# Attention with a deferred softmax normalisation and an earlier weight-quantisation schedule, one post-LN layer on 8 cores

## Chip, cores and metric

One Trainium2 chip, one program on all 8 NeuronCores. The time is device microseconds of the slowest core. The cores share no data while the kernel runs: cores 0 to 3 work on batch element 0, cores 4 to 7 on batch element 1, and each core owns 2048 of the 8192 tokens of its element.

## What is computed

One transformer layer with the layer norm behind each residual sum:

```python
qkv = x @ w_qkv + b_qkv                      # x: (2, 8192, 2048), 16 heads of 128
scores = einsum('bqhd,bkhd->bhqk', q * SCALE, k)
attn = softmax(scores, axis=-1)
out = einsum('bhqk,bkhd->bqhd', attn, v)
x = layernorm(x + out @ w_proj + b_proj)

def quantize(w):                              # ternary weights
    gamma = mean(abs(w))                      # one number for the whole matrix
    return clip(round(w / (gamma + 1e-8)), -1, 1)
hidden = sigmoid(x @ quantize(w1).T) * (x @ quantize(w2).T)
x = layernorm(x + hidden @ quantize(w3).T)
```

w1 and w2 are 5632x2048, w3 is 2048x5632. The quantised weights depend on nothing that attention computes, so the kernel prepares them beside attention.

## The kernel before

Everything is written in raw engine programs: each phase is a block with one instruction stream per engine (tensor, scalar, vector, gpsimd, sync), and the order within a stream is the order of the code. Engines meet only at semaphores (t_a, t_b, t_c, t_q raised by TensorE, s_a by ScalarE, v_a, v_b, v_q, v_q2 by VectorE, and one ring per stream of DMAs). A block starts with `barrier`, which makes an engine wait for every count of the earlier blocks, the rings of DMAs included.

Phases in order: K and V projections for all 8192 tokens (to HBM scratch kscr, vscr), Q projection of the core's 2048 tokens (into qtsb), attention, output projection with layer norm, then the feed-forward part in two halves of 1024 tokens.

Attention (lines 540 to 773) runs over 16 heads h and, in each, two query halves qp of 1024 queries: 32 groups, g = 2h + qp. A group goes through 64 key chunks kc of 128 keys. TensorE makes the scores of a chunk (line 638, two matmuls of 512 columns into one of two tiles ps_s), ScalarE takes the exponential (line 696, ps_s to exs), and TensorE multiplies it with V (line 649, into po) and sums it with a column of ones (line 653, into row 0 of pl), always one chunk behind the scores. The last chunk's four matmuls are lines 660 and 663.

At the end of a group the sums are inverted and spread over the partitions. VectorE takes two reciprocals (lines 707, 708: pl to rlsb). TensorE spreads them with a one-row matmul (line 669) into ps_s[0]. VectorE copies that to rbsb (line 711) and multiplies both halves of po with it (line 714, into qtsb), raising v_b. Only then may TensorE start the next group, whose kc = 0 waits for v_b (line 634). ps_s, po and pl together fill PSUM, and the tiles pl have one partition each.

The weights are quantised on VectorE between groups, in 136 chunks of 128 rows by 2048 (or 1536) columns, in two passes. Pass 1 sums absolute values (line 724, L724 in the profile, wbuf2 to racc) of 17 chunks behind the second group of each of the heads 0 to 7. At the end of head 7 the totals give the three factors gi3, through two tiny matmuls (lines 677, 681), and TensorE may start head 8 only when they are there (line 626, v_q at NQ + 3). Pass 2 quantises (lines 754, 758, 762) 17 chunks behind the second group of each of the heads 8 to 15, and GpSimd stores them. GpSimd issues the loads of both passes three ahead of VectorE. SyncE loads K and V of a head two heads ahead.

The change touches the PSUM tiles pl, the lists q1_of_h and q2_of_h, and the attention streams of TensorE and VectorE. GpSimd's, ScalarE's and SyncE's streams stay as they are.

## Time and profile before

| | us |
|---|---|
| runs, median of 2 | 10211.64 (9977.26 to 10446.01) |
| the profiled execution's own time | 9977.26 |
| its span on the slowest core (core 0) | 9975.7 |
| spans of the eight cores | 9926.5 to 9975.7 |
| TensorE busy, core 0 | 8313.6 (83% of the span) |
| ScalarE busy | 2833.3 (28%) |
| VectorE busy | 2009.4 (20%) |

The page counts a matmul as busy from its start to its modelled end. The engines work side by side, so the shares don't add up to 100%. What stands in the row of a stage says more than the mean over the whole span, since the stages have different limits. Times within the text are microseconds from the start of the span of core 0.

### The profile page before, as it was taken

The page shows a single profiled execution, that of the slowest core. Times are in us where ns is not written, and L with a number is a line of the kernel's source. Part 1 is how long each engine was busy: PE and PEld are TensorE (multiplying, and loading weights), DVE is VectorE, ACT ScalarE, POOL GpSimd, SP SyncE. Part 2 cuts the span into 40 slices and gives each one's busy share as a digit, 9 for nine tenths or more (in the row PEclk, how much of TensorE's full clock was granted, in tenths as well). Part 3 has the DMA queues.
Part 4 walks back from the last instruction along what each step waited for, and adds up shares of the span by engine and source line. Part 5 has one row for each costly group of instructions (what it writes and reads, how often), then busy time and mean ns, then how long its engine had stood idle before and what let it go on. Part 6 is the DMA issues. An engine that isn't in the chain of part 4 may idle for free. (4 is left out here: it accounts for less than half of the span.)

```text
span 9975.7 us, 92282 instructions; the slowest of 8 cores (9926.5 to 9975.7 us)
## 1 busy us (share of the span) xinstructions
PE 8313.6 (83%) x31982; PEld 2850.2 (29%) x31982; DVE 2009.4 (20%) x1975; ACT 2833.3 (28%) x2856; POOL 730.0 (7%) x1119
## 2 busy tenths in 40 slices
PE   6999699988999999979999999956499876399773
PEld 2444244432222222222222222212144322144221
DVE  1111111111222222220333333343300001100002
ACT  1111111123555555545555555510000000000000
POOL 2111111100000000000111111111100000000000
PEclk9999899999999999989999999978799999699997
DMA  5333433443222222220333333279733222533223
GB/s 88 69 69 70 83 70 72 75 67 64 89 89 87 85 83 83 75 82 21 125 125 125 125 125 117 98 145 123 114 78 79 49 71 65 124 77 68 56 70 103
DMA packets 1174111, 868.24 MB, mean 87 GB/s; under 512 B 925857, under 2 KB 1056929, under 8 KB 1140897
## 3 DMA queue, kind: packets, MB, share of 16 engines
q0 software_dynamic: 312704, 488.71, 21.6%
q1 hardware_dynamic: 860962, 373.62, 15.2%
q8 instruction: 276, 4.52, 0.2%
q14 instruction: 169, 1.38, 0.1%
HBM read 679.52 MB, written 186.65 MB: 87 GB/s over the span
## 5 line engine op out<-in xcount | busy, mean ns | idle before, releaser
L696 ACT ACTIVATE exs<-ps_s,negc 128x1024 bf16<-128x1024 f32 x2048 | 2278.6, 1114 | 1800.5 <-PE ps_s L638 1800.4
L649 PE MATMUL po<-exs,vh 128*128 128x512 bf16 x4032 | 1583.0, 393 | 17.4 <-ACT exs L696 17.4
L653 PE MATMUL pl<-exs,ones_bf 128*1 128x512 bf16 x4032 | 1546.3, 384 | 0.0
L638 PE MATMUL ps_s<-qtsb,kh 128*128 128x512 bf16 x4096 | 1287.1, 399 | 116.4 <-DVE qtsb L714 86.1
L270 PE MATMUL pk<-xg,wkv 128*128 128x512 bf16 x4096 | 928.9, 381 | 153.2 <-DMA xg<-xb 153.2
L1183 PE MATMUL px<-hidden,w3t 128*128 128x512 bf16 x2816 | 708.7, 386 | 242.8 <-DMA w3t<-w3qs 240.2
L298 PE MATMUL pv<-wkv,xg 128*128 128x512 bf16 x4096 | 894.6, 380 | 10.4 <-DVE vsb L346 10.4
L1060 PE MATMUL px<-ysbh,w1t 128*128 128x512 bf16 x2816 | 626.1, 381 | 215.7 <-DMA w2t<-w2qs 215.7
L653 PEld LDWEIGHTS pl<-exs,ones_bf 128*1 128x1 bf16 x4032 | 318.6, 79 | 1220.7 <-issue 1220.7
L316 ACT ACTIVATE ksb<-pk,bkrs 128x512 bf16<-128x512 f32 x256 | 176.0, 687 | 1666.2 <-PE pk L270 1485.2
L649 PEld LDWEIGHTS po<-exs,vh 128*128 128x128 bf16 x4032 | 391.1, 97 | 896.8 <-issue 889.3
L707 DVE RECIPROCAL rlsb<-pl 1x512 f32<-1x512 f32 x32 | 107.1, 3346 | 2652.6 <-PE pl L663 2652.6
L1069 PE MATMUL px<-ysbh,w2t 128*128 128x512 bf16 x2816 | 622.1, 379 | 0.0
L270 PEld LDWEIGHTS pk<-xg,wkv 128*128 128x128 bf16 x4096 | 386.5, 98 | 641.5 <-issue 207.4
L298 PEld LDWEIGHTS pv<-wkv,xg 128*128 128x128 bf16 x4096 | 399.0, 98 | 498.4 <-issue 25.6
L1183 PEld LDWEIGHTS px<-hidden,w3t 128*128 128x128 bf16 x2816 | 242.2, 98 | 716.0 <-issue 524.3
L1060 PEld LDWEIGHTS px<-ysbh,w1t 128*128 128x128 bf16 x2816 | 276.3, 98 | 553.6 <-issue 224.2
L638 PEld LDWEIGHTS ps_s<-qtsb,kh 128*128 128x128 bf16 x4096 | 241.0, 99 | 645.2 <-issue 645.2
L1085 ACT ACTIVATE s1s<-px 128x1024 bf16<-128x1024 f32 x88 | 90.1, 1024 | 1097.5 <-PE px L1069 1097.4
L61 POOL DMA_DIRECT2D xg<-xb x512 | 272.0, 634 | 1551.1 <-PE pv L298 1538.5
L335 DVE TENSOR_REDUCE knmax<-pn 1x1 f32<-1x512 f32 x256 | 173.8, 679 | 1025.0 <-PE pn L281 988.2
L1069 PEld LDWEIGHTS px<-ysbh,w2t 128*128 128x128 bf16 x2816 | 275.5, 98 | 332.2
(118 smaller groups left out, 3943.4 us busy)
## 6 DMA issues: line engine op xcount, KB each, us to landing
wbuf<-w POOLq DMA_DIRECT2D x240, 1024.0 KB, 7.6
xg<-xb POOLq DMA_DIRECT2D x512, 128.0 KB, 7.3
kscr<-ksb SPq DMA_DIRECT2D x256, 128.0 KB, 1.8
vscr<-vsb SPq DMA_DIRECT2D x1024, 32.0 KB, 1.6
kh<-kscr SPq DMA_DIRECT2D x16, 2048.0 KB, 8.0
wp<-wproj POOLq DMA_DIRECT2D x64, 512.0 KB, 9.8
wbuf<-w POOLq DMA_DIRECT2D x32, 768.0 KB, 7.7
w1qs<-wqb POOLq DMA_DIRECT2D x44, 512.0 KB, 5.5
```

The source lines that it names most:

```text
L61: e.dma_start(out=out, in_=in_, **kw).then_inc(cc.h, 16)
L270: mm = e.matmul(pk[idx % 2][:], wkv[:, dc * 2048 + h_l * 128:dc * 2048 + (h_l + 1) * 128], xg[s % 2][:, dc * 512:(dc + 1) * 512], start=(d ...
L298: mm = e.matmul(pv[jdx % 2][:], xg[s % 2][:, dc * 512 + kc * 128:dc * 512 + (kc + 1) * 128], wkv[:, dc * 2048 + 1024 + g4l * 512:dc * 2048 ...
L316: e.activation(ksb[idx % 2][:], pk[idx % 2][:], AF.Identity, bias=bkrs[:, h:h + 1], scale=RS)
L335: rm = e.reduce_max(knmax[0:1, col:col + 1], pn[idx % 2][0:1, :], axis=AX)
L638: mm = e.matmul(ps_s[kc % 2][:, q2 * 512:(q2 + 1) * 512], kh[h % 2][:, kc * 128:(kc + 1) * 128], qtsb[:, h * TOK + qp * 1024 + q2 * 512: h ...
L649: e.matmul(po[q2][:], vh[h % 2][:, p * 128:(p + 1) * 128], exs[p % 4][:, q2 * 512:(q2 + 1) * 512], start=(p == 0), stop=False)
L653: mm = e.matmul(pl[q2][0:1, :], ones_bf[:, 0:1], exs[p % 4][:, q2 * 512:(q2 + 1) * 512], start=(p == 0), stop=False)
L696: s_a.inc(e.activation(exs[kc % 4][:], ps_s[kc % 2][:], AF.Exp, bias=negc[:, h:h + 1]))
L1060: e.matmul(px1[jc % 2][:, q2 * 512:(q2 + 1) * 512], w1t[jg % 2][:, dc * 512 + jc2 * 128: dc * 512 + jc2 * 128 + 128], ysbh[:, dc * 1024 + ...
L1069: mm = e.matmul(px2[jc % 2][:, q2 * 512:(q2 + 1) * 512], w2t[jg % 2][:, dc * 512 + jc2 * 128: dc * 512 + jc2 * 128 + 128], ysbh[:, dc * 10 ...
L1183: mm = e.matmul(px3[dcw][:, q2 * 512:(q2 + 1) * 512], w3t[n % 4][:, dcw * 128:(dcw + 1) * 128], hidden[:, hc * 1024 + q2 * 512: hc * 1024 ...
```

## The change

Four edits, all within attention:

1. The tiles pl get 128 partitions instead of one. They keep their two PSUM banks.
2. The matmuls that spread the reciprocals of group g write into pl and no longer into ps_s[0], and they stand in the next group: behind its scores of kc = 0 and kc = 1. The wait for v_b moves there too, ahead of the first product with V. Groups 13 and 31 are exceptions. Group 13's spread stands at the end of head 6 (there line 682), group 31's behind the last head.
3. VectorE copies pl to rbsb in two pieces of 512 columns instead of one of 1024.
4. Pass 1 takes 23, 23, 23, 23, 22 and 22 chunks behind heads 0 to 5, the factors are made at the end of head 6, and pass 2 takes 17 chunks behind each of the heads 7 to 14.

```diff
-                pl = [... psum_tensor(f"pl{i}", [1, 512], F32))
+                pl = [... psum_tensor(f"pl{i}", [128, 512], F32))
...
-                q1_of_h = [list(range(h_ * 17, (h_ + 1) * 17)) if h_ < 8 else []
-                           for h_ in range(H)]
-                q2_of_h = [list(range((h_ - 8) * 17, (h_ - 7) * 17)) if h_ >= 8
-                           else [] for h_ in range(H)]
+                _q1c = [23, 23, 23, 23, 22, 22] + [0] * 10
...
+                q2_of_h = [list(range((h_ - 7) * 17, (h_ - 6) * 17))
+                           if 7 <= h_ <= 14 else [] for h_ in range(H)]
...
-                            if h == 8:
+                            if h == 7:
                                 e.wait_ge(v_q.h, b[v_q] + NQ + 3)
...
-                                    if kc == 0 and g >= 1:
-                                        e.wait_ge(v_b.h, b[v_b] + g)
...
+                                    if kc == 1 and g >= 1:
+                                        if g != 14:
+                                            e.wait_ge(v_a.h, b[v_a] + g)
+                                            for q2 in range(2):
+                                                mm = e.matmul(
+                                                    pl[q2][:], ones_fr[0:1, :],
+                                                    rlsb[0:1, q2 * 512:(q2 + 1) * 512],
+                                                    start=True, stop=True)
+                                            t_c.inc(mm)
+                                        e.wait_ge(v_b.h, b[v_b] + g)
...
-                                e.wait_ge(v_a.h, b[v_a] + g + 1)
-                                for q2 in range(2):
-                                    mm = e.matmul(ps_s[0][:, q2 * 512:(q2 + 1) * 512],
...
-                            if h == 7:
+                            if h == 6:
+                                e.wait_ge(v_a.h, b[v_a] + 14)
...
                                 e.wait_ge(v_q.h, b[v_q] + NQ + 1)
-                                e.wait_ge(v_b.h, b[v_b] + 16)
...
-                                vsync(e, e.tensor_copy(rbsb[:], ps_s[0][:]))
+                                e.tensor_copy(rbsb[:, 0:512], pl[0][:])
+                                vsync(e, e.tensor_copy(rbsb[:, 512:1024],
+                                                       pl[1][:]))
...
-                                if h == 7:
+                                if h == 6:
```

TensorE between groups 0 and 1, before: the last four products of group 0, the spread of the reciprocals (from rlsb), the scores of the next group (ps_s, from kh0), and its first product.

```order
L660 MATMUL po1<-exs3,vh0 128x512
L663 MATMUL pl1<-exs3,ones_bf 1x512
L669 MATMUL ps_s0<-rlsb,ones_fr 128x512 [waits v_a]
L669 MATMUL ps_s0<-rlsb,ones_fr 128x512
L638 MATMUL ps_s0<-qtsb,kh0 128x512 [waits v_b]
L638 MATMUL ps_s0<-qtsb,kh0 128x512
L638 MATMUL ps_s1<-qtsb,kh0 128x512 x2
L649 MATMUL po0<-exs0,vh0 128x512 [waits s_a]
```

The same place after the change.

```order
L672 MATMUL po1<-exs3,vh0 128x512
L675 MATMUL pl1<-exs3,ones_bf 1x512
L640 MATMUL ps_s0<-qtsb,kh0 128x512 x2
L640 MATMUL ps_s1<-qtsb,kh0 128x512 x2
L651 MATMUL pl0<-rlsb,ones_fr 128x512 [waits v_a]
L651 MATMUL pl1<-rlsb,ones_fr 128x512
L661 MATMUL po0<-exs0,vh0 128x512 [waits v_b,s_a]
```

The four matmuls of the scores have moved ahead of the spread and wait for nothing, and the wait for v_b now stands on the first product with V.

VectorE at the end of attention, before: the last group's copy and products (rbsb, qtsb), then the first of 17 chunks of pass 2 (gi: the factors, tq and wqb: the quantised chunk).

```order
L711 COPY rbsb<-ps_s 128x1024 [waits t_c]
L714 TENSOR_TENSOR qtsb<-po,rbsb 128x512 [waits v_s]
L714 TENSOR_TENSOR qtsb<-po,rbsb 128x512
L754 TENSOR_SCALAR tq<-wbuf_2,gi 128x2048 [waits v_b,r_q22,r_q2s1]
L758 TENSOR_SCALAR tq<-wbuf_2,gi 128x2048 [waits v_s]
L762 TENSOR_TENSOR wqb_1<-tq 128x2048 [waits v_s]
```

The same place after the change.

```order
L727 COPY rbsb<-pl 128x512 [waits t_c]
L728 COPY rbsb<-pl 128x512
L732 TENSOR_TENSOR qtsb<-po,rbsb 128x512 [waits v_s]
L732 TENSOR_TENSOR qtsb<-po,rbsb 128x512
L577 UNCONDITIONAL_BRANCH [waits v_b]
```

No chunk of pass 2 is left behind the last group, and the block ends there.

## Rows read from the trace of the kernel before

**Rows 1.** Stages, core 0: us; PE, PEld, DVE, ACT, POOL busy; clock, DMA share, GB/s.

```profile
2385.00:4525.00 2140.00, 1875.36 (x6281) 506.10 (x6281) 453.90 (x257) 1153.16 (x1037) 73.83 (x139) 0.90 0.27 86
...
6520.00:6640.00 120.00, 15.32 (x58) 5.93 (x59) 65.30 (x59) 3.35 (x4) 33.18 (x37) 0.56 0.76 208
```

**Rows 2.** Timeline of core 0 around the end of group 6.

```profile
3296.39 3.35 DVE L707 RECIPROCAL rlsb<-pl 1x512 f32<-1x512 f32 x1 [58.32 <-PE pl L663]
...
3303.09 3.75 PE L669 MATMUL ps_s<-rlsb,ones_fr 1*128 1x512 f32 x4 [6.81 <-DVE rlsb L708]
...
3306.95 1.22 DVE L711 COPY rbsb<-ps_s 128x1024 f32<-128x1024 f32 x1 [4.00 <-PE ps_s L669]
...
3309.71 1.86 PE L638 MATMUL ps_s<-qtsb,kh 128*128 128x512 bf16 x4 [2.87 <-DVE qtsb L714]
...
3312.08 0.58 PE L649 MATMUL po<-exs,vh 128*128 128x512 bf16 x1 [0.50 <-ACT exs L696]
```

**Rows 3.** The reciprocal that opens each group's end: groups 7, 15 and 16.

```profile
3422.61 3.35 DVE L707 RECIPROCAL rlsb<-pl 1x512 f32<-1x512 f32 x1 [113.05 <-PE pl L663]
4432.73 3.35 DVE L707 RECIPROCAL rlsb<-pl 1x512 f32<-1x512 f32 x1 [112.96 <-PE pl L663]
4614.95 3.35 DVE L707 RECIPROCAL rlsb<-pl 1x512 f32<-1x512 f32 x1 [112.29 <-PE pl L663]
```

**Rows 4.** Stretch of core 0, TensorE alone: busy, granted clock, DMA share, GB/s.

```profile
3318.00:3320.00 2.00, 2.00 (x8) 0.96 0.00 0
```

**Rows 5.** Scores of four chunks of group 7, two at each clock level.

```profile
3314.16 1.03 PE L638 MATMUL ps_s<-qtsb,kh 128*128 128x512 bf16 x2
...
3317.12 1.03 PE L638 MATMUL ps_s<-qtsb,kh 128*128 128x512 bf16 x2
...
3319.31 0.60 PE L638 MATMUL ps_s<-qtsb,kh 128*128 128x512 bf16 x2
...
3321.00 0.60 PE L638 MATMUL ps_s<-qtsb,kh 128*128 128x512 bf16 x2
```

**Rows 6.** The stall at the end of head 7: VectorE, then TensorE.

```profile
4497.74 1.75 DVE L724 TENSOR_REDUCE racc<-wbuf 128x1 f32<-128x1536 f32 x1 [0.31 <-DMA wbuf<-w]
...
4503.13 1.87 PE L638 MATMUL ps_s<-qtsb,kh 128*128 128x512 bf16 x4 [0.73 <-DVEq L748]
```

**Rows 7.** The end of attention and the start of the output projection, core 0.

```profile
6508.20 3.35 DVE L707 RECIPROCAL rlsb<-pl 1x512 f32<-1x512 f32 x1 [113.10 <-PE pl L663]
...
6520.09 1.29 DVE L714 TENSOR_TENSOR qtsb<-po,rbsb 128x512 bf16<-128x512 f32 x2
...
6602.44 0.96 DVE L762 TENSOR_TENSOR wqb<-tq 128x1536 bf16<-128x1536 bf16 x1
...
6612.44 45.42 SPq L61 DMA_DIRECT2D xm<-xm  x9
6622.67 11.99 PE L877 MATMUL pp<-qtsb,wp 128*128 128x512 bf16 x48 [104.02 <-DMA wp<-wproj]
```

**Rows 8.** The start of attention, core 0: last copy before it, first load, first product.

```profile
2395.73 0.17 DVE L499 COPY negc<-pnc 128x16 f32<-128x16 f32 x1 [0.82 <-PE pnc L504]
2397.09 0.32 SPq L61 DMA_DIRECT2D kh<-kscr  x1
...
2428.81 0.59 PE L649 MATMUL po<-exs,vh 128*128 128x512 bf16 x1 [1.78 <-ACT exs L696]
```

**Rows 9.** The end of group 0.

```profile
2539.06 3.35 DVE L707 RECIPROCAL rlsb<-pl 1x512 f32<-1x512 f32 x1 [143.16 <-PE pl L663]
```

**Rows 10.** Stretches as in the fourth group, at the starts of attention and of the projection.

```profile
2434.00:2436.00 2.00, 2.00 (x8) 0.97 1.14 217
6624.00:6626.00 2.00, 2.00 (x7) 0.58 1.72 161
```

**Rows 11.** Pass 1 behind head 0: first and last chunk.

```profile
2678.43 2.29 DVE L724 TENSOR_REDUCE racc<-wbuf 128x1 f32<-128x2048 f32 x1 [0.18 <-DVE qtsb L714]
...
2730.61 2.29 DVE L724 TENSOR_REDUCE racc<-wbuf 128x1 f32<-128x2048 f32 x1 [0.27 <-DMA wbuf<-w]
```

**Rows 12.** Groups by form: a VectorE copy of 512 columns out of PSUM.

```profile
L189 DVE COPY bvb<-pstp 128x512 f32<-128x512 f32 x4 | 2.8, 692 | 9.6 <-PE pstp L181 9.6
```

More of the change, by code:

```diff
@@ L566, in build @@
                 NW = 44 * 128 * 2048
-                q1_of_h = [list(range(h_ * 17, (h_ + 1) * 17)) if h_ < 8 else []
-                           for h_ in range(H)]
-                q2_of_h = [list(range((h_ - 8) * 17, (h_ - 7) * 17)) if h_ >= 8
-                           else [] for h_ in range(H)]
+                _q1c = [23, 23, 23, 23, 22, 22] + [0] * 10
+                q1_of_h = []
+                _qa = 0
+                for h_ in range(H):
+                    q1_of_h.append(list(range(_qa, _qa + _q1c[h_])))
+                    _qa += _q1c[h_]
+                q2_of_h = [list(range((h_ - 7) * 17, (h_ - 6) * 17))
+                           if 7 <= h_ <= 14 else [] for h_ in range(H)]
                 b = snap()
@@ L683, in _ @@
                                                  start=True, stop=True))
+                        e.wait_ge(v_a.h, b[v_a] + 32)
+                        for q2 in range(2):
+                            mm = e.matmul(pl[q2][:], ones_fr[0:1, :],
+                                          rlsb[0:1, q2 * 512:(q2 + 1) * 512],
+                                          start=True, stop=True)
+                        t_c.inc(mm)
                     @blk.scalar
```

9 lines of the change are left out of this document (5 added, 4 removed).

## The prediction

> **What bounds the kernel now.** I read the spans of the cores first: all eight lie within 50 us of each other, so core 0 stands for the chip. Then I read the stages. In the first half of attention TensorE is busy for 1875 of 2140 us, ScalarE for 1153 and VectorE for 454 [rows 1], and the second half looks alike, so TensorE's order of work sets the time there, and only what lets TensorE start sooner, or run at the higher of its two clock levels for longer, can pay. Behind attention comes a stretch of 120 us in which TensorE has 15 us of work and its granted clock is 0.56 of full speed [rows 1].
>
> The timeline gives three kinds of gap within attention. The first stands at the end of every group [rows 2]. Behind the last matmul of group 6 TensorE idles 6.81 us for the two reciprocals, spreads them for 3.75 us, idles 2.87 us for copy and products, makes four scores matmuls (1.86 us), and waits 0.50 us for the exponential. The first product with V starts at 3312.08, which is 15.69 us after the reciprocal's start at 3296.39. The second gap is at the end of head 7: from one reciprocal to the next it takes 182.22 us [rows 3] instead of the usual 126.22 (3296.39 to 3422.61) [rows 2, 3]. TensorE can't begin head 8 before 4503.13, because 17 chunks of pass 1 and the factors stand ahead of it on VectorE [rows 6]. The third is the tail: the last group's products end at 6521.38, then come 17 chunks of pass 2 to 6603.40, then the stores must land, and the next phase's first load is issued at 6612.44 [rows 7].
>
> The 32 reciprocals lie between 2539.06 and 6508.20 [rows 7, 9]. That is 3969.14 us in 31 intervals. Without the long one there remain 3786.92 us in 30 intervals, or 126.23 us each.
>
> **The group boundary.** Edit 2 leaves the chain of reciprocals, spread, copy and products as it is, and takes the four scores matmuls and the wait for the first exponential from behind it. They now run while the reciprocals are taken. The first product with V can start where the scores start now, 13.32 us after the reciprocal's start (3309.71 less 3296.39) [rows 2]. Queued behind the new wait for the reciprocals is only work that needs po or pl, both of which VectorE still reads; ScalarE has both exponentials done within the 6.81 us. Nothing is delayed by the move.
>
> Edit 3 turns a copy of 1.22 us [rows 2] into two of 512 columns. One such copy alone takes 0.69 us [rows 12], so two take 1.38 at most. The pair of products of the same width takes 1.29 [rows 7]. I take 0.1 us more. The bounds are 0.07 and 0.16, under 3 us of difference over all groups. By the Trainium skill (VectorE: DVE Perf Modes, "The TRN2 errata"), each instruction out of PSUM pays a fixed 120 cycles, an estimate of 0.13 us for the second copy. The rows' bounds, 0.07 and 0.16, lie around that; the sum would be 1 us less of a gain by it. With my 0.1 the first product starts 13.4 us after the reciprocal.
>
> How long is it from the first product to the next reciprocal? The trace has one group that starts just as all will after the change, with both exponentials ready: group 0. Its first product starts at 2428.81 [rows 8] and its reciprocal at 2539.06 [rows 9]: 110.25 us. So an interval would be 13.4 + 110.25 = 123.65 us.
>
> A part of this is the clock. After each gap TensorE runs at 1.2 GHz for a while. At group 6's end the clock comes back just after 3318 (0.96 over 3318 to 3320) [rows 4], 8.4 us after the restart at 3309.71 and 6 us after the first product. In group 0 it came back just after 2434 [rows 10], 5.3 us after the first product. At the projection's start, with matmuls in one unbroken row from 6622.67 [rows 7], it came back within 3.3 us (0.58 over 6624 to 6626) [rows 10]. The low clock costs 0.43 of its time here: a chunk takes 2.96 us (3314.16 to 3317.12) instead of 1.69 (3319.31 to 3321.00) [rows 5]. I expect 3.5 to 5.5 us of it after a restart without the half-microsecond pause, towards the short end, which makes 109.5 to 110.3 us, and take 109.6. The interval is then 13.4 + 109.6 = **123.0 us**. The bounds are 122.7 and 124.2 (a return 6.8 us after the product).
>
> The rule of the Trainium skill (TensorE: Matmul & The Clock Gate, "What's actually happening") is that the slow state is the default and recent activity releases it. By that rule it is the unbroken row of matmuls that counts, and the trace agrees: 3 to 5 us in the unbroken row and 8.4 us with the pause of 0.50 us in it.
>
> By the moved work alone, 15.69 less 13.4, the gain would be 2.3 us an interval; the rest of my 3.2 is the shorter low clock, as group 0 and the projection's start show it.
>
> The gain is 126.23 − 123.0 = 3.2 us in 30 intervals, **97 us** (61 to 106 by the bounds).
>
> **The end of head 6.** The stall moves to group 13, with no chunk ahead of it. There VectorE ends its products 13.3 us after the reciprocal. The three totals, two tiny matmuls and factors take what they take now, from 4499.49 (4497.74 + 1.75) to 4503.13, 3.64 us [rows 6]. Since TensorE waits for them before head 7, its scores stay behind the chain here: 1.87 + 0.50 us more until the first product. 13.3 + 3.6 + 2.4 + 110 makes 129.3 us. Against 182.2 this gains **53 us** (51 to 54).
>
> What must hide the 17 chunks that stood there is the 113 us that VectorE is idle in a group [rows 3]. Pass 1 takes 54.5 us for 17 chunks (2678.43 to 2732.90) [rows 11], 3.2 us each, so 23 take 74 us. Even without the three that are loaded ahead it is 77. Some 39 us are left before the next reciprocal. The loads share the DMA queues with K and V of a later head in the kernel before too, so their pace already has that in it. If that cover were gone, each us over it would stall TensorE six times.
>
> **The tail.** Pass 2 ends behind head 14, where the 82 us of its 17 chunks (6521.38 to 6603.40 in the tail now) [rows 7] fit into the same 113 us. The last group's products are then the last work of the block. From there to the first load of the next block it is now 91.06 us (6521.38 to 6612.44) [rows 7]. The start of attention shows what such a change of blocks takes with nothing outstanding: 1.2 us from the end of the copy (2395.90) to the first load (2397.09) [rows 8]. Gain: **90 us** (85 to 91). What is late next is the load of w_proj, 10.2 us from the first issue to the first matmul (6612.44 to 6622.67) [rows 7], as before. Nothing in the later phases changes.
>
> **Sum.** 97 + 53 + 90 = 240 us. The profiled execution took 9977.26 us, its span being 9975.7, so the forecast is **9738 us**. The median of the two runs shown, 10211.64, lies 234 us above that execution, half-way to a run of 10446. I predict against the profiled one.
>
> **Rivals.**
>
> 1. The low clock stays as long after a restart as it does now, 8.4 us from the first matmul. Then an interval is 13.4 + 108.0 + 0.43 x 8.4 = 125.0 us, where 108.0 is 110.25 less 0.43 x 5.3. Only 37 us come from the boundaries, 180 in all: 9797 us. For it speaks that the four matmuls ahead of the chain and the spread still leave pauses of some 6 and 3 us; against it, group 0 [rows 8 to 10].
> 2. A part of the 90 us comes back. If the eight cores reach the projection closer together and its weight loads slow each other, or the cores that now finish early wait, half of the gain could go: 9783 us. Against it: all cores show the same stages now, and DMA was already at 0.76 in the tail [rows 1].
> 3. Slower: the 23 chunks don't fit. VectorE takes the next reciprocal late, and TensorE, which in a group's end waits for nothing else, stalls in six groups. To eat the other gains, each of the six stalls must be 40 us, so that 23 chunks take 153 us, 6.6 us a chunk. The measured pace is 3.2 [rows 11], and it starts to matter at 4.9 us. At 7 us a chunk the time would be 9738 + 6 x (161 − 113), or 10026 us.
>
> **How the numbers follow.** The forecast gets 0.72, rival 1 0.14, rival 2 0.11, and rival 3 0.03. The forecast's bounds reach from about 9724 (all gains at their upper end) to 9781, and executions differ by some 0.3%, 30 us. With rivals 1 and 2 the range is 9700 to 9800. A change of 2% is about what a measurement of this kernel can tell from none; here it is 200 us, so faster means under 9778 us. The forecast lies 40 us on that side, rival 1 on the other, and rival 2 on the edge. That gives 0.82 for faster, 0.15 for within 2%, and 0.03 for slower.
>
> **What would show it.** In the profile after: about 123 us between reciprocals; TensorE's four scores matmuls directly behind a group's last product; the first product with V about 13.4 us behind the reciprocal's start, and the clock back within 5.5 us of it; one interval of about 129 us between groups 13 and 14 and none of 182; the first load of the projection 1 to 2 us behind VectorE's last product; pass 1 done some 75 us behind each of six heads. The prediction is wrong if the intervals stay above 124.5 us, if a reciprocal waits for a chunk of pass 1, or if TensorE's idle time before the projection is above 30 us.

## The result, and the profile after

| | before | after |
|---|---|---|
| median of all runs, us | 10426.7 (13 runs) | 10214.23 (14 runs) |
| lowest, us | 9977.26 | 9734.5 |
| ratio after / before | | 0.9746, 95% interval 0.9726 to 0.9766 |
| span of core 0 in the profiled execution, us | 9975.7 | 9733.8 |

The changed kernel is faster by 2.5%. The forecast was 9738. The comparison rests on five executions of after, from 9734.5 to 9750.51 us, and three of before, from 9977.26 to 10012.81, since in all the others, which set both medians, the cores of one die or both ran at a lower granted clock, as they did in many executions of the experiments too (the two longest, the first of one_ahead and the first of ones128, took 16385 and 23688 us). The profile of after comes from an execution of 10238.4 us, whose late cores are 4 to 7. All rows of after below are from core 0, whose span was 9733.8 us and whose mean granted clock was 0.932.

On core 0 the gain is 9975.7 − 9733.8 = 241.9 us; I had summed 240. It is divided as follows.

The end of a group comes first. This is the timeline of core 0 of after around the end of group 2; the rows are those of [rows 2] in their new order, and the last is the next group's reciprocal.

```profile
2776.77 1.04 PE L640 MATMUL ps_s<-qtsb,kh 128*128 128x512 bf16 x4
2776.94 3.35 DVE L723 RECIPROCAL rlsb<-pl 1x512 f32<-1x512 f32 x1 [35.49 <-PE pl L675]
...
2783.64 3.75 PE L651 MATMUL pl<-rlsb,ones_fr 1*128 1x512 f32 x4 [5.84 <-DVE rlsb L724]
...
2787.50 0.69 DVE L727 COPY rbsb<-pl 128x512 f32<-128x512 f32 x1 [4.00 <-PE pl L651]
2788.11 0.68 DVE L728 COPY rbsb<-pl 128x512 f32<-128x512 f32 x1
2788.89 1.29 DVE L732 TENSOR_TENSOR qtsb<-po,rbsb 128x512 bf16<-128x512 f32 x2
...
2790.43 0.58 PE L661 MATMUL po<-exs,vh 128*128 128x512 bf16 x1 [3.04 <-DVE qtsb L732]
...
2899.68 3.35 DVE L723 RECIPROCAL rlsb<-pl 1x512 f32<-1x512 f32 x1 [109.51 <-PE pl L675]
```

The four scores matmuls start directly behind the group's last product, at the high clock (1.04 us for four, where they took 1.86 behind the chain). The chain of reciprocals, spread, copies and products is as long as it was. The first product with V no longer waits for an exponential: it is released by VectorE's products. It starts 2790.43 − 2776.94 = 13.49 us after the reciprocal, where it was 15.69. From it to the next reciprocal, at 2899.68, it takes 109.25 us. The interval is 122.74 us. Its mean over all boundaries but one is 122.9, where it was 126.23. Of these 3.3 us 2.2 come from the work that was moved (15.69 less 13.49) and 1.1 from the time between the first product and the next reciprocal (110.54 us before, 109.42 after, in the mean).

TensorE alone in short stretches of core 0 of after, as in [rows 4] (busy, granted clock, DMA share, GB/s).

```profile
2792.00:2794.00 2.00, 2.00 (x6) 0.52 0.00 0
```

The higher of the two clock levels, 2.4 GHz, is back at about 2793.9, which is 3.5 us after the first product (3.3 to 4.2 over the 30 boundaries of this kind). Before the change it was 6 us (5.1 to 6.4).

The whole of attention stands in one row of the view of one line, the first reciprocal of each group (duration in ns; first and last start).

```profile
L723 DVE RECIPROCAL rlsb<-pl x32: 3345/3346/3346, 2531.1 to 6347.4; 1x512 f32<-1x512 f32 x32
```

6347.4 − 2531.1 = 3816.3 us, against 3969.14 before [rows 7, 9]. One of the 31 intervals is the one behind head 6. Its ends, and what happens between, on core 0 of after:

```profile
4128.70 3.35 DVE L723 RECIPROCAL rlsb<-pl 1x512 f32<-1x512 f32 x1 [109.68 <-PE pl L675]
...
4145.28 1.86 PE L640 MATMUL ps_s<-qtsb,kh 128*128 128x512 bf16 x4 [0.63 <-DVEq L766]
...
4257.59 3.35 DVE L723 RECIPROCAL rlsb<-pl 1x512 f32<-1x512 f32 x1 [112.68 <-PE pl L675]
```

Here the totals follow VectorE's products at once, TensorE's scores wait for the factors as at the end of head 7 before [rows 6], and the interval is 128.89 us instead of 182.22. The other 30 share 3687.4 us, 122.9 each.

What had to hide the longer pieces of pass 1 still hides them: behind head 0 the first and the last of 23 chunks lie 74.0 us apart, from the first start to the last end, and the next reciprocal comes 35.5 us later (2741.45 to 2776.94), released by TensorE. The rows answer to [rows 11].

```profile
2667.45 2.29 DVE L742 TENSOR_REDUCE racc<-wbuf 128x1 f32<-128x2048 f32 x1 [0.18 <-DVE qtsb L732]
...
2739.16 2.29 DVE L742 TENSOR_REDUCE racc<-wbuf 128x1 f32<-128x2048 f32 x1 [0.63 <-DMA wbuf<-w]
```

The tail on core 0 of after, as in [rows 7].

```profile
6359.36 1.29 DVE L732 TENSOR_TENSOR qtsb<-po,rbsb 128x512 bf16<-128x512 f32 x2
6362.55 1.30 SPq L61 DMA_DIRECT2D xm<-xm  x3
...
6371.91 4.42 PE L895 MATMUL pp<-qtsb,wp 128*128 128x512 bf16 x10 [14.06 <-DMA wp<-wproj]
```

From the end of the last products, 6360.65, to the first load of the projection it is 1.9 us, where it was 91.06. TensorE's idle time before the projection fell from 104.02 to 14.06 us, and what ends it is still the load of w_proj. The stage of attention says the same, in the columns of [rows 1]: TensorE is busy for 1939 of 2140 us instead of 1875, at a mean clock of 0.93 instead of 0.90.

```profile
2377.00:4517.00 2140.00, 1939.44 (x6607) 529.19 (x6607) 529.61 (x332) 1213.16 (x1092) 101.58 (x173) 0.93 0.31 99
```

So 152.8 us come from between the first and the last reciprocal and 90.0 us from TensorE's idle time ahead of the projection, 243 together. The phases ahead of the first reciprocal were 8 us shorter, and those from the projection's first matmul to the end took 3361.9 us, 9 more than before. Both are within what the same code shows from one execution to the next, below.

### The profile page after: what moved, and what is told of

Read it like the earlier page. It is cut to its first block and busy times, and to the rows that moved or that the text cites. A ratio compares the mean times of both kernels' runs of the same rounds, so it can differ in the third digit from the quotient of the medians.

```text
span 10236.9 us, 92313 instructions; the slowest of 8 cores (9712.5 to 10236.9 us)
## 1 busy us (share of the span) xinstructions
PE 8770.1 (86%) x31982; PEld 2916.2 (28%) x31982; DVE 2010.8 (20%) x2007; ACT 2833.2 (28%) x2856; POOL 740.0 (7%) x1119
## 5 line engine op out<-in xcount | busy, mean ns | idle before, releaser
L661 PE MATMUL po<-exs,vh 128*128 128x512 bf16 x4032 | 1630.6, 404 | 93.5 <-DVE qtsb L732 91.2
L665 PE MATMUL pl<-exs,ones_bf 128*1 128x512 bf16 x4032 | 1589.0, 394 | 0.0
L270 PE MATMUL pk<-xg,wkv 128*128 128x512 bf16 x4096 | 1089.1, 429 | 148.8 <-DMA xg<-xb 148.8
L298 PE MATMUL pv<-wkv,xg 128*128 128x512 bf16 x4096 | 1051.5, 428 | 7.6 <-DVE vsb L346 7.6
L270 PEld LDWEIGHTS pk<-xg,wkv 128*128 128x128 bf16 x4096 | 420.4, 106 | 755.1 <-issue 689.2
L298 PEld LDWEIGHTS pv<-wkv,xg 128*128 128x128 bf16 x4096 | 435.5, 107 | 614.9 <-issue 530.9
L1103 ACT ACTIVATE s1s<-px 128x1024 bf16<-128x1024 f32 x88 | 90.2, 1024 | 1097.4 <-PE px L1087 1097.4
```

Of the source, the lines that this page charges most:

```text
L270: mm = e.matmul(pk[idx % 2][:], wkv[:, dc * 2048 + h_l * 128:dc * 2048 + (h_l + 1) * 128], xg[s % 2][:, dc * 512:(dc + 1) * 512], start=(d ...
L298: mm = e.matmul(pv[jdx % 2][:], xg[s % 2][:, dc * 512 + kc * 128:dc * 512 + (kc + 1) * 128], wkv[:, dc * 2048 + 1024 + g4l * 512:dc * 2048 ...
L661: e.matmul(po[q2][:], vh[h % 2][:, p * 128:(p + 1) * 128], exs[p % 4][:, q2 * 512:(q2 + 1) * 512], start=(p == 0), stop=False)
L665: mm = e.matmul(pl[q2][0:1, :], ones_bf[:, 0:1], exs[p % 4][:, q2 * 512:(q2 + 1) * 512], start=(p == 0), stop=False)
```

## The experiments

Times are of the profiled execution, and rows of core 0, where nothing else is said. "The reciprocals" are the first of each group, and their interval is the length of a group with its end. In the experiments from the pause on the lowest times of the unchanged kernel before, taken beside them on the same chips, were 9980 to 10006 us. Beside the first three its lowest was 10409.39 us, so their times aren't set against it, only their rows against those of the profile before.

### Each half of the change alone

**The schedule alone** (edit 4 in the kernel before; the chain stays as it was):

```diff
-                q1_of_h = [list(range(h_ * 17, (h_ + 1) * 17)) if h_ < 8 else []
+                _q1c = [23, 23, 23, 23, 22, 22] + [0] * 10
...
-                            if h == 8:
+                            if h == 7:
                                 e.wait_ge(v_q.h, b[v_q] + NQ + 3)
```

> The kernel before with the new schedule of the quantisation alone (edit 4). My theory, that the terms add and are independent: the intervals between reciprocals stay at 126.2 us, the one of 182.2 us becomes about 129.9 us (126.2 plus 3.6 for the factors), and the tail of 91 us becomes 2 us. That is 52 + 89 = 141 us less, some 1.4%. The rival theory, that the earlier passes of quantisation give something back (chunks that make a reciprocal late, or weight loads of the projection that collide), expects intervals behind heads 0 to 5 above 126.5 us or a projection that starts later, and less than 100 us in all.

**The deferred spread alone** (edits 1 to 3, the old lists):

```diff
-                                    if kc == 0 and g >= 1:
-                                        e.wait_ge(v_b.h, b[v_b] + g)
...
+                                    if kc == 1 and g >= 1:
+                                        if g != 16:
+                                            e.wait_ge(v_a.h, b[v_a] + g)
...
                             if h == 7:
+                                e.wait_ge(v_a.h, b[v_a] + 16)
```

> The kernel after with the old schedule of the quantisation (edits 1 to 3 alone). My theory: intervals of 122.9 us instead of 126.2 at 30 boundaries, 99 us less in all (1.0%), with the stall at the end of head 7 (182 us) and the tail (91 us) as before. If the clock came back no sooner after a restart than in the kernel before, and only the four scores matmuls and the wait for the exponential were saved, the intervals would be 123.9 to 125.0 us and the gain 37 to 70 us.

They took 9845.22 and 9883.4 us. The reciprocals of the two kernels, the schedule alone first.

```profile
L711 DVE RECIPROCAL rlsb<-pl x32: 3345/3346/3346, 2521.3 to 6432.1; 1x512 f32<-1x512 f32 x32
```

```profile
L719 DVE RECIPROCAL rlsb<-pl x32: 3344/3346/3346, 2540.1 to 6408.5; 1x512 f32<-1x512 f32 x32
```

With the schedule alone the intervals stay at 126.2 us, but for some of 124.0 to 125.9 behind groups 16 to 21, the one behind head 6 is 129.87, and TensorE's idle time ahead of the projection is 14.5 us instead of 104.0. Attention gains 58.3 us (3969.1 less 3910.8) and the tail 90. With the deferred spread alone all intervals but one are 122.9 us, and the stall behind head 7 stays, with an interval of 180.7. It gains 100.7 us in attention (3969.1 less 3868.4), where I had summed 97. The tail stays: TensorE is idle for 110.3 us ahead of the projection, 6 more than before.

The two gains in attention add up to 159 us; the whole change has 152.8. The 6 us that are left are the shorter intervals behind groups 16 to 21, which the whole change doesn't have. There the clock comes back sooner. This is the first product behind the end of group 17, and the clock around it.

```profile
4684.91 0.58 PE L653 MATMUL po<-exs,vh 128*128 128x512 bf16 x1 [0.50 <-ACT exs L700]
```

```profile
4684.00:4686.00 2.00, 1.50 (x4) 0.52 0.77 146
```

It is back 1.0 us after the first product here (0.52 over 4684 to 4686, and 1.00 from then on), and 3.0 to 5.7 us after it at the five other places, where most boundaries of this kernel have 5.8 to 6.4, all with the same matmuls and the same pause of 0.50 us. What brings it back sooner there is open. Otherwise the terms are independent, and each is where I had put it.

**Only the tail undone** (the change, with pass 2 behind heads 8 to 15 again):

```diff
-                q2_of_h = [list(range((h_ - 7) * 17, (h_ - 6) * 17))
-                           if 7 <= h_ <= 14 else [] for h_ in range(H)]
+                q2_of_h = [list(range((h_ - 8) * 17, (h_ - 7) * 17))
+                           if 8 <= h_ <= 15 else [] for h_ in range(H)]
```

> The kernel after with pass 2 behind heads 8 to 15 as before, pass 1 and the factors early. Theory: only the tail comes back, 89 us (stores of the last chunks included), and the intervals in attention stay at 122.9 and 128.9 us. The rival, that the early pass 2 costs something within attention (its loads and stores beside K and V), expects less than 89 us between the two kernels, by what the early pass had cost.

It took 9841.88 us. The projection's first matmuls:

```profile
6464.51 10.84 PE L895 MATMUL pp<-qtsb,wp 128*128 128x512 bf16 x39 [104.21 <-DMA wp<-wproj]
```

Attention is as long as with the whole change (3816.3 us). TensorE's idle time ahead of the projection is 104.21 again, 90.15 more than the 14.06 with the whole change. Core 0's span is 106.5 us longer, though, 14 of it in the phases behind, where the two kernels have the same code: 3375.8 us against 3361.9. Over all kernels of this part the same phases took 3351.8 to 3375.8 us. A difference of spans is thus uncertain by some 20 us, and that is why the terms are read from the places where they arise. Rival 2, by which a part of the 90 us comes back, has nothing for it but the 9 us by which these phases were longer in after than in before, and this kernel, with the old tail, has the longest of all.

### What brings the clock back

The forecast took 0.9 of the 3.2 us that it gave each boundary from a sooner return of the clock, and gave the matmuls' unbroken row behind the restart as the reason. Two kernels break the row or change its place.

**A pause put in** (the products of the second chunk wait for the third exponential):

```diff
-                                        e.wait_ge(s_a.h, eb + p + 1)
+                                        e.wait_ge(s_a.h,
+                                                  eb + (3 if p == 1 and kc == 2 else p + 1))
```

> The kernel after with a pause put back behind the restart: the second chunk's products with V wait for the third exponential, not only the second, so TensorE stops for about 1.5 us some 3 us after each group's first product. Theory, that only an unbroken row of matmuls brings the clock back: it comes back 6.5 to 8.5 us after the first product instead of 3.5, and the interval is 13.4 + 108 + 1.5 + 0.43 x (5.3 to 6.8) = 125.2 to 125.8 us. Rival, that the time after the restart alone decides: the clock is back 3.5 us after the first product in spite of the pause, and the interval is 124.1 us.

It took 9866.59 us. The end of group 2 on its core 0, then stretches of TensorE as above.

```profile
2784.11 3.35 DVE L723 RECIPROCAL rlsb<-pl 1x512 f32<-1x512 f32 x1 [37.05 <-PE pl L675]
...
2797.61 0.58 PE L661 MATMUL po<-exs,vh 128*128 128x512 bf16 x1 [3.04 <-DVE qtsb L732]
...
2802.08 0.58 PE L661 MATMUL po<-exs,vh 128*128 128x512 bf16 x1 [1.36 <-ACT exs L712]
...
2910.19 3.35 DVE L723 RECIPROCAL rlsb<-pl 1x512 f32<-1x512 f32 x1 [112.83 <-PE pl L675]
```

```profile
2806.00:2808.00 2.00, 2.00 (x7) 0.78 0.00 0
```

The chain is as in the change (13.50 us to the first product), the pause is 1.36 us long, and the interval is 126.08 us (126.2 in the mean). The clock is back at about 2806.9, 9.3 us after the first product and 4.8 us after the pause. At 29 of the 30 boundaries of this kind it is 9.0 to 9.6 us. So the rival, by which the return comes 3.5 us after the product whatever stands behind it, is refuted there. At the one behind group 14 the return is at 3.4 us and the interval 124.0 us, the rival's own numbers, with the same pause. The theory's direction is right for nearly all, and its size too small: it costs 3.3 us an interval, more than I expected. With 5.8 us more at the low clock, at 0.43 of the time, 2.5 us of it are the clock and some 0.8 the pause itself. Why the return takes 9.3 us and not the 6.5 to 8.5 of the expectation isn't settled.

**Less work ahead of the chain** (only the first chunk's scores are ahead; the second's follow the wait for v_b):

```diff
-                                    for q2 in range(2):
-                                        mm = e.matmul(
-                                            ps_s[kc % 2][:, q2 * 512:(q2 + 1) * 512],
...
-                                    t_a.inc(mm)
                                     if kc == 1 and g >= 1:
...
                                         e.wait_ge(v_b.h, b[v_b] + g)
+                                    for q2 in range(2):
+                                        mm = e.matmul(
+                                            ps_s[kc % 2][:, q2 * 512:(q2 + 1) * 512],
...
+                                    t_a.inc(mm)
```

> The kernel after, but only the scores of chunk 0 go ahead of the chain; those of chunk 1 stand behind the wait for v_b again, so that the restart is scores, then products, with no pause. Theory (unbroken row): the clock is back 3 to 6.8 us after the restart, the interval is 13.4 + 108.4 + 0.43 x (3.4 to 6.8) = 123.3 to 124.7 us. Rival, that what shortened the low clock was matmuls ahead of the chain, or that the restart must begin with products: the clock stays low for 8.4 us as in the kernel before, and the interval is 125.4 us.

It took 9772.9 us. The restart at the end of group 2 and the stretch in which the clock returns, then the same for group 5.

```profile
2784.03 1.01 PE L650 MATMUL ps_s<-qtsb,kh 128*128 128x512 bf16 x2 [2.94 <-DVE qtsb L732]
```

```profile
2786.00:2788.00 2.00, 2.00 (x6) 0.72 0.00 0
```

```profile
3152.98 1.01 PE L650 MATMUL ps_s<-qtsb,kh 128*128 128x512 bf16 x2 [2.94 <-DVE qtsb L732]
```

```profile
3157.00:3159.00 2.00, 2.00 (x5) 0.50 0.87 242
```

In the first the unbroken row begins with two scores matmuls at 2784.03, and the clock is back about 3.1 us later. At 25 boundaries it is back 2.9 to 4.7 us behind the restart, but at five, of which the second is one, 6.0 to 6.3 us, with an unbroken row there too; these five have the longest intervals, 124.3 to 124.6 us. The interval is 123.5 us in the mean, 0.6 above the change's, for 1 us more of work behind the restart. So most of the gain doesn't rest on how much stands ahead of the chain.

Counted from the restart alike, the return comes 3.3 to 4.2 us behind it in the change, 2.9 to 4.7 or 6.0 to 6.3 us here, and 3.0 us at the projection's start [rows 7, 10], all with nothing in between. Where a wait interrupts TensorE it is 8.4 us at the end of group 6 before (7.5 to 8.7 at the others) [rows 2, 4], 9.0 to 9.6 us with the longer pause, and 8.9 us in group 0, where four scores matmuls at 2425.16 and a wait of 1.78 us stand ahead of the first product [rows 8, 10]. Against this stand the one boundary of the pause kernel with 3.4 us and four of the schedule alone, with 3.4 to 6.7 us in spite of the wait. So an interruption mostly goes with a later return, but it isn't all that decides, and what else does wasn't tested. By the rule of the Trainium skill that the prediction weighed (TensorE: Matmul & The Clock Gate, "What's actually happening") recent activity releases the slow state; most of these boundaries agree, and the exceptions aren't explained by it as I used it.

### The cover of pass 1

**Pass 1 behind three heads** (45, 45 and 46 chunks), to test rival 3 where it must decide:

```diff
-                _q1c = [23, 23, 23, 23, 22, 22] + [0] * 10
+                _q1c = [45, 45, 46] + [0] * 13
```

> The kernel after with pass 1 in 45, 45 and 46 chunks behind heads 0 to 2. Theory: VectorE takes a chunk in 3.2 us as before, so 45 take 144 us where 109.6 us are idle; three intervals grow from 122.9 to about 158 us, 105 us more in all, all other intervals are unchanged. If the pace fell below that once the loads ran on without a break (the slower rival of the prediction), the three intervals would be above 170 us.

It took 10174.27 us. I read it on core 2, whose mean granted clock, 0.913, is the highest of the eight. There all intervals but three and the one behind head 6 are 122.7 to 123.8 us, close to the change's. Under the row stands what ends VectorE's wait before a reciprocal, and how often.

```profile
L723 DVE RECIPROCAL rlsb<-pl x32: 3345/3345/3346, 2675.7 to 6615.1; 1x512 f32<-1x512 f32 x32
its engine sat idle before it (us, times) until:
  PE pl L675: 2517.7, 29
  DVE racc L742: 0.8, 3
```

Three of 32 reciprocals are released by a chunk of pass 1, and not by TensorE: the stall that rival 3 described. Their intervals are about 163 us, 40 more (expected 158), and attention is 3939.4 − 3816.3 = 123 us longer. So the mechanism is real, at 45 chunks and 3.3 us a chunk. The change's 23 chunks take 74 of the 109.5 us that VectorE is idle in a group of the changed kernel (122.9 less 13.4), and they cost nothing.

### Past the change: the sums

What is left at a group's end is the chain itself. It exists because the sums stand in one partition: a matmul with a column of ones. With a 128 by 128 matrix of ones the sums stand in all partitions at once, and the spread and its copy aren't needed.

**Ones of 128 columns, the reciprocal straight from PSUM:**

```diff
-                                            mm = e.matmul(pl[q2][0:1, :],
-                                                          ones_bf[:, 0:1],
+                                            mm = e.matmul(pl[q2][:],
+                                                          ones_bb[:],
...
+                                e.reciprocal(rbsb[:, 0:512], pl[0][:])
+                                vsync(e, e.reciprocal(rbsb[:, 512:1024],
+                                                      pl[1][:]))
```

> The kernel after, with the sums taken by a 128x128 tile of ones instead of 128x1, so that they stand on all partitions and VectorE takes the reciprocals straight to rbsb: no spread, no copy. The chain to the first product falls from 13.4 to about 8.3 us. Theory (the chain is what bounds the boundary): intervals of 118 us if loading 128 columns of ones costs TensorE nothing more, 120.5 us if the 19 ns by which the two weight loads differ (98 and 79 ns) come on top in each of the 128 products of a group. Rival, that the bound is elsewhere: intervals stay near 122.9 us or rise.

It took 9084.55 us (another execution 9075.62), and attention 3164.1 from first to last reciprocal. The chain at one group's end:

```profile
2738.65 3.36 DVE L703 RECIPROCAL rbsb<-pl 128x512 f32<-128x512 f32 x1 [15.25 <-PE pl L668]
...
2745.32 1.29 DVE L708 TENSOR_TENSOR qtsb<-po,rbsb 128x512 bf16<-128x512 f32 x2
```

The chain is 8.0 us long instead of 13.4, as reckoned; the reciprocal of 512 columns takes 3.36 us whether in 1 or 128 partitions. But the intervals are 101 to 102.4 us, not 118 to 120.5. Some 16 us a group more went than the shorter chain accounts for. That asked for a kernel with the ones alone.

**Ones of 128 columns, and nothing else** (the chain, the spread and the copies stay as in the change):

```diff
-                                            mm = e.matmul(pl[q2][0:1, :],
-                                                          ones_bf[:, 0:1],
+                                            mm = e.matmul(pl[q2][:],
+                                                          ones_bb[:],
```

> The kernel after with the sums taken by the 128x128 tile of ones, and nothing else: reciprocals of row 0, spread and copies stay. The run with ones on 128 columns and a shorter chain had intervals of 102 us where 118 to 120.5 were expected. Theory: the rest came from the product's weights. With weights of one column a matmul starts 0.31 us after the one before it, with 128 columns throughout 0.22 us, so a chunk falls from 1.69 to about 1.43 us and the interval by 64 x 0.26 = 16.6 us, to 106.3 us. Rival, that the shorter chain alone did it (an idle time short enough for the clock to stay up for most of the boundary): the interval stays at 122 to 123 us.

It took 9238.45 us.

```profile
L725 DVE RECIPROCAL rlsb<-pl x32: 3344/3345/3347, 2513.4 to 5831.8; 1x512 f32<-1x512 f32 x32
```

3318.4 us, or 107 an interval; most of the saving is in the steady row of matmuls and has nothing to do with the boundary. The theory had 106.3, and the rival, the shorter chain alone, 122 to 123. The shorter chain is worth the other 5 us (107 here, 102 in the version before). A chunk within a group, in the timeline with the weight loads (PEld), first of the changed kernel and then of this one:

```profile
3001.07 0.38 PE L661 MATMUL po<-exs,vh 128*128 128x512 bf16 x1
...
3001.37 0.08 PEld L665 LDWEIGHTS pl<-exs,ones_bf 128*1 128x1 bf16 x1 [0.24 <-issue]
3001.38 0.38 PE L665 MATMUL pl<-exs,ones_bf 128*1 128x512 bf16 x1
3001.68 0.10 PEld L661 LDWEIGHTS po<-exs,vh 128*128 128x128 bf16 x1 [0.23 <-issue]
```

```profile
3001.25 0.38 PE L663 MATMUL po<-exs,vh 128*128 128x512 bf16 x1
3001.25 0.10 PEld L667 LDWEIGHTS pl<-exs,ones_bb 128*128 128x128 bf16 x1
3001.47 0.38 PE L667 MATMUL pl<-exs,ones_bb 128*128 128x512 bf16 x1
3001.47 0.10 PEld L663 LDWEIGHTS po<-exs,vh 128*128 128x128 bf16 x1
```

In the first, these loads stand at the start of their own matmuls, behind the matmul before, and a matmul and its neighbour start 0.31 us apart where one of the two has the single column. The two others of the six steps of a chunk, from scores to scores and from scores to the first product, are 0.22 us long in the steady row of this kernel too. In the second kernel a load stands one matmul ahead, under the one that is running, and all of them can start 0.215 us apart. A chunk takes 1.43 us in the mean instead of 1.69, and 64 chunks of 0.26 us less make the 16 us. The mean is over 6 x 0.215 = 1.29 us since TensorE now often waits for ScalarE ahead of the first product, which then starts 0.15 us behind the end of the exponential. That step is mostly 0.27 or 0.44 us long, and in the stretch shown chunks take 1.30 and 1.56 us in turn. "Busy" doesn't show it: the duration printed for one matmul is 0.38 to 0.39 us in both.

**The reciprocal off the path** (ones of 128 columns; VectorE copies pl and po out of PSUM, raises v_b, and inverts and multiplies in SBUF beside the next group):

```diff
+                                    e.tensor_copy(
+                                        rbsb[:, q2 * 512:(q2 + 1) * 512],
+                                        pl[q2][:])
...
+                                    mm = e.tensor_copy(
+                                        pob[:, q2 * 512:(q2 + 1) * 512],
+                                        po[q2][:])
+                                v_b.inc(mm)
+                                e.wait_ge(v_b.h, v_b.n)
+                                vsync(e, e.reciprocal(rbsb[:], rbsb[:]))
```

> The kernel after with the sums on all partitions (128x128 ones) and the normalisation off TensorE's path: VectorE copies pl and po out of PSUM (four copies of 512 columns, 2.6 us) and raises v_b; reciprocal and product follow in SBUF while the next group runs. The first product comes about 2.9 us behind the last one of the group before plus the scores, so TensorE idles 2 us instead of 5.8 + 3.0. If the clock then stays high, the intervals are 2.9 + 108 = 111 us, and 113.4 with a slower weight load; if it still falls, about 2 us more. That is 9.5 to 12 us less in 31 intervals than in the kernel after, about 9740 - 330 = 9410 us. Rival: the clock falls at each boundary and stays low as long as now, or the longer work of VectorE behind v_b (8 us) makes pass 1 or 2 late; then the intervals are 115 us or more and the time is above 9500 us.

Its two best executions took 8913.27 and 8924.95 us; the rows are of core 0 of another, with a span of 8897.7 us. A group's end, then TensorE in the stretch behind the end of the group before it and behind this one.

```profile
2988.82 1.29 DVE L705 COPY rbsb<-pl 128x512 f32<-128x512 f32 x2 [85.46 <-PE pl L669]
...
2991.41 6.55 DVE L714 RECIPROCAL rbsb<-rbsb 128x1024 f32<-128x1024 f32 x1
...
2991.56 0.38 PE L655 MATMUL po<-exs,vh 128*128 128x512 bf16 x1 [1.98 <-ACT exs L693]
```

```profile
2897.00:2899.00 2.00, 1.78 (x6) 0.50 0.00 0
...
2991.00:2993.00 2.00, 1.44 (x7) 1.00 0.92 377
```

The boundary costs TensorE 1.98 us of idle time. Behind this one the clock doesn't fall (1.00), but that is the exception: at 20 of the 24 boundaries with this idle time it falls behind the restart, as at the one before (0.50 over 2897 to 2899), and is back 3.5 to 4.7 us after the first product. Where it falls the interval is mostly 95.7 to 95.9 us, at the four where it doesn't 94.0 to 94.2. The expectation, 9410 us, was made before the effect of the ones was known. From the 107 us of ones_only the first product's earlier start takes 10.75 us (2.74 us behind the first copy instead of 13.49), and the shorter low clock some 0.4, which makes the measured 95.7. Behind the heads 7 to 11, though, the intervals are 101 to 102 us, and VectorE's timeline at one of these shows why:

```profile
4251.83 1.22 DVE L761 TENSOR_TENSOR wqb<-tq 128x2048 bf16<-128x2048 bf16 x1
4253.23 1.29 DVE L705 COPY rbsb<-pl 128x512 f32<-128x512 f32 x2 [0.17 <-DVE wqb L761]
```

The copy out of PSUM is released by a chunk of pass 2, and no longer by TensorE: rival 3's mechanism. 17 of the wide chunks take 89 to 91 us there, 65 of them work, and most of the rest waits for the stores; with VectorE's 11 us at the group's end that is more than 95.7. Behind heads 12 to 14, with narrower chunks in them, they take 83 to 85 us, and these intervals stay at 94.2 to 95.9 us.

**The chunks spread over all groups** (12 or 11 of pass 1 behind groups 0 to 11, 8 of pass 2 behind groups 14 to 30, the factors behind group 13):

```diff
-                _q1c = [23, 23, 23, 23, 22, 22] + [0] * 10
+                _q1c = [12] * 4 + [11] * 8 + [0] * 20
...
+                q2_of_g = [list(range((g_ - 14) * 8, (g_ - 13) * 8))
+                           if 14 <= g_ <= 30 else [] for g_ in range(2 * H)]
```

> The kernel with copies out of PSUM and the normalisation off the path, and the chunks of pass 1 and 2 spread over all groups (12 or 11 behind groups 0 to 11, 8 behind groups 14 to 30) instead of every other one. In the run before it the intervals were 95.7 us, but some 102 us in pass 2: there 17 chunks (82 us) and VectorE's own 11.5 us leave nothing of 95.7. Theory: all intervals but the one with the factors are 95.7 us and attention takes 30 to 40 us less than before, some 8870 us in all. Rival, that the loads and stores of pass 2 themselves slow the groups: intervals between 96 and 100 us in every group of pass 2, and no gain.

It took 8886.93 us, spans of 8836.4 to 8885.4. Attention from the first copy to the last, and what ends VectorE's wait before it.

```profile
L705 DVE COPY rbsb<-pl x64: 678/686/692, 2513.8 to 5482.6; 128x512 f32<-128x512 f32 x64
its engine sat idle before it (us, times) until:
  PE pl L669: 1662.2, 32
```

All 32 are released by TensorE, the intervals are 93.9 to 96.0 us (108.9 at the factors), and attention takes 39 us less than in the version before (3007.1 to 2968.2, from the first copy of the first group to that of the last). The rival, intervals of 96 to 100 us all through pass 2, is refuted. This version beats both kernels: its 8886.93 us is 1090 below the lowest time of before and 848 below the lowest of after. It is one execution, so no interval stands beside it.

## Why the prediction was right, and where it was not

**The group boundary: right.** "With my 0.1 the first product starts 13.4 us after the reciprocal": 13.49. "I expect 3.5 to 5.5 us of it after a restart, towards the short end": 3.5. "Which makes 109.5 to 110.3 us, and take 109.6": 109.25. The interval came out at 122.9 instead of 123.0, and 30 of them gained 100 us instead of 97. I had divided the 3.2 us of an interval into 2.3 for the moved work and 0.9 for the clock; they are 2.2 and 1.1 of 3.3. The price of the low clock, 0.43 of its time, is borne out by the schedule alone: at the boundary shown the clock is back 5.2 us sooner than at most, and the interval is 124.0 us, 2.2 less. Rival 1 (125.0 us) is refuted by the same rows. The reason that I gave for the sooner return, the unbroken row, holds at most boundaries and isn't the whole of it, as the exceptions above show, so that part of the mechanism is argued. My measure for it was crooked too: I compared 5.3 us in group 0, counted from the first product, with 8.4 us at group 6, counted from the scores. From the scores on, with the wait between them, group 0 has 8.9 us, as this row of the kernel before says.

```profile
2425.16 1.86 PE L638 MATMUL ps_s<-qtsb,kh 128*128 128x512 bf16 x4 [29.54 <-DMA vh<-vscr]
```

So only the projection's start, at 3.0 us, spoke for the unbroken row, and that the term of 3.5 to 5.5 us held is in part luck. The second copy costs 0.69 + 0.60 where one took 1.22, 0.07 us more, the lower of the two bounds. The fixed 120 cycles of the Trainium skill (VectorE: DVE Perf Modes, "The TRN2 errata"), an estimate of 0.13 us, are more than that; nothing here hangs on it.

**The end of head 6: right.** 128.89 us for 129.3. The gain is 53.3 us, forecast 53. The schedule alone shows it apart from the rest.

**The cover of pass 1: right.** 74.0 us for 23 chunks, the number of the prediction, and no reciprocal waits for one. What is left is 35.5 us and not 39, since the change makes the group itself shorter, which I had not taken off. Rival 3 was tested from the other side: with 45 chunks the stall appears in the size that the pace makes, and the pace hardly rises (3.3 us a chunk). For pass 2 I took 82 us from the tail, whose chunks are in part narrower; behind heads 7 to 11 its 17 chunks take 89 to 91 us, which fits all the same.

**The tail: right.** 90.0 us less idle time ahead of the projection, forecast 90; putting back pass 2's place alone brings back 90.15. The load of w_proj is what is late next, as said.

**The phases behind: within the noise.** "Nothing in the later phases changes" holds as far as can be told: they came out 9 us longer, and the same code differs by up to 24 us between kernels.

**What the forecast was compared with: wrong.** The sum gives 9738, and the five executions compared took 9734.5 to 9750.51. The three of before have a mean of 9995.8 us and these five one of 9742.1, 253.7 less; 9977.26, from which I subtracted, was the lowest of the three. But the median of all 14 is 10214.23, far above my upper end of 9800. The step that failed is "I predict against the profiled one". I had the warning in hand: "The median of the two runs shown, 10211.64, lies 234 us above that execution, half-way to a run of 10446." I read it as one stray run, and it was the common case: 10 of 13 times of before lie that far up. Subtracting 240 from the median shown wouldn't have been right either (9972), since a median of two says nothing of how often that happens: with 13 runs it is 10426.7. What the range lacked is this spread, 480 us between the lowest time and the median of after and 449 between those of before, with which no term of the change has anything to do. The chances were on the ratio, and faster by over 2%, at 0.82, is what happened.

**What I took as given and shouldn't have.** Each term used the 1.69 us a chunk as TensorE's own pace. 0.26 us of it, 15%, come from a stationary operand of one column (the operand that is loaded into TensorE ahead of a matmul; here the column of ones). That doesn't touch the forecast, as both kernels have it, but the largest gain of this kernel (509 us of core 0's span, against the change's 242) stood in a row that I had read only for its sum.

## What to carry to other kernels

Read a boundary for what stands behind the restart as well as for the wait itself: work that can run before a serial chain should, and behind the chain TensorE should find everything ready: with a wait of half a microsecond there the clock came back 5.1 to 6.4 us after the first product, and without it after 3.3 to 4.2. Work hidden on another engine is free until its pace times its count reaches the interval, and shortening the interval (here from 122.9 to 95.7 us) brings that point nearer, so spread it evenly. And divide a long row of matmuls by its count before taking its pace as given: 0.31 us from start to start for 512 columns, against 0.215 with another operand, doesn't show in the busy time. Look at more than one boundary before telling what the clock does at them: single ones here differ from most by 3 us and more.

## What the runs showed of the hardware that I had not expected

- A one-column bf16 stationary operand among 128-column ones makes its own matmul and the one behind it start 0.31 us after the last, and with 128 columns throughout it is 0.215 us, for the same 512 moving columns: 9733.8 us of span against 9224.8. In the rows the weight loads run under the matmul before where all have 128 columns, and the loads next to the single column don't. The Trainium skill (TensorE: Matmul & The Clock Gate, "Weight-path perf modes — Fast Weight Load (FWL) and DoubleRow") says that the fast load is used where the number of weights is 128. The rows agree in that the change from 1 to 128 columns is what speeds up the row; whether the mode is the reason, or the loads' place one matmul ahead, no run here separates.
- With 128 columns throughout, chunks of 1.30 and 1.56 us come in turn, and the difference stands ahead of the first product, which waits for ScalarE's exponential. Why the wait alternates wasn't tried.
- The clock's return, counted from the first product, is at 3.3 to 4.2 us in an unbroken row, 5.1 to 6.4 with a pause of 0.50 us ahead of that product, and 9.0 to 9.6 with one of 1.36 us some 3 us behind it. Single boundaries with the same matmuls and pauses break this: 1.0 us in the schedule alone, 3.4 with the longer pause. After an idle time of 1.98 us the clock fell at 20 of 24 boundaries and stayed up at four.
- A reciprocal of 512 float32 columns out of PSUM takes 3.35 us in one partition and 3.36 in 128, and one of 1024 columns out of SBUF takes 6.55 us.
